# Where the edge counts of a two-layer graph kernel are made: in the second loop, or ahead of it

## The reference, cut to what matters

```python
h = relu(layernorm(x))
Q, K, V = h @ Wq + bq, h @ Wk + bk, h @ Wv + bv          # 8 heads of 16
scores = sum(Q[dst] * K[src], -1) * scale + (edge_attr @ We + be)
p = exp(scores - segment_max(scores, dst)[dst])
x = x + (segment_sum(p * V[src], dst) / segment_sum(p, dst)) @ Wo + bo

h = relu(layernorm(x))
h = logmap0(h) @ W.T + b
deg = count(dst) + count(src);  dinv = deg ** -0.5
out = segment_sum(h[src] * dinv[src] * dinv[dst], dst)
x = x + expmap0(out)
```

## Time and profile before

| what | value |
|---|---|
| median of 3 runs | 884.59 us |
| the profiled execution, its span | 885.71 us, 883.5 us |
| PE, PE weight loads | 778.6 us (88%), 604.3 us (68%) |
| DVE, ACT, POOL | 695.8 us (79%), 529.5 us (60%), 558.7 us (63%) |
| first product of the attention sums, of the counted sums | 81.7 us, 652.5 us |
| mean granted clock of PE | 0.942 of full speed |

### The profile page before, as it was taken

One profiled execution on the slowest core, in us unless ns is written; L12 is line 12 of the kernel. 1 busy time (PEld: TensorE's weight loads), 2 busy tenths in 40 slices (PEclk: granted clock), 3 DMA queues, 4 the chain that ended last, 5 costly groups with the idle time before them and its releaser, 6 DMA issues.

```text
span 883.5 us, 20988 instructions
## 1 busy us (share of the span) xinstructions
PE 778.6 (88%) x5179; PEld 604.3 (68%) x5179; DVE 695.8 (79%) x2576; ACT 529.5 (60%) x1376; POOL 558.7 (63%) x581
## 2 busy tenths in 40 slices
PE   5658978999889999999999999987479999999995
PEld 2336756767667777777777777775358888787875
DVE  8846865878657787877877877776999898999984
ACT  4477745666545776766667667642856556464641
POOL 0077775777756777777777777750067767666762
PEclk9958989999979999999999999996789999999998
DMA  5653464555544445445445445442132222222221
GB/s 173 203 150 100 121 126 108 122 131 124 117 94 110 136 122 139 122 127 138 124 125 139 125 124 140 124 110 77 45 83 64 70 57 68 59 71 55 70 57 49
DMA packets 107213, 94.96 MB, mean 107 GB/s; under 512 B 39836, under 2 KB 91265, under 8 KB 107169
## 3 DMA queue, kind: packets, MB, share of 16 engines
q0 software_dynamic: 25088, 65.05, 27.5%
q1 hardware_dynamic: 82089, 29.51, 13.6%
HBM read 83.35 MB, written 11.15 MB: 107 GB/s over the span
## 4 chain that ended last, share of the span: by engine, by line
PE 35%; DVE 22%; issue 14%; POOL 10%; DMA 8%; SPq 5%; ACT 3%; DVEq 2%; POOLq 1%
POOL kv L816 9%; PE ps_q L1852 7%; PE ps_r L1872 5%; PE ps_s L1829 5%; DVE wv L1501 3%; DMA kv<-kv_tab,idx 3%; DMA qwin<-q_tab 3%; DVE fwd_reset L1500 3%; PE ps_r L2030 3%; PE ps_c L1821 2%; PE ps_f L1907 2%; PE ps_s L1839 2%; DVE ST L1500 1%; SPq L593 1%; ACT ST L1621 1%
## 5 line engine op out<-in xcount | busy, mean ns | idle before, releaser
L816 POOL DMA_INDIRECT kv<-kv_tab,idx x416 | 401.4, 965 | 187.9 <-issue 114.4
L859 POOL DMA_INDIRECT kv<-hs_tab,idx x160 | 156.9, 981 | 122.8 <-DMA hs_tab<-qkv 54.2
L1621 ACT ACTIVATE ST<-ps_s,imj 128x512 f32<-128x512 f32 (+1 forms) x128 | 77.1, 603 | 139.4 <-PE ps_s L1839 139.0
L1852 PE MATMUL ps_q<-qwin,ST 128*128 128x128 f32 x832 | 129.5, 298 | 19.1 <-DMA qwin<-q_tab 15.8
L1852 PEld LDWEIGHTS ps_q<-qwin,ST 128*128 128x128 f32 x832 | 111.9, 202 | 30.3 <-issue 26.1
L1092 DVE TENSOR_TENSOR prod<-kv,ps_q 128x512 f32<-128x512 f32 (+1 forms) x128 | 71.9, 576 | 67.9 <-PE ps_q L1852 43.8
L1604 ACT ACTIVATE S<-iota,nloc 128x128 f32<-128x128 f32 x384 | 121.9, 388 | 0.0
L1872 PE MATMUL ps_r<-wv,S 128*128 128x137 f32 x832 | 114.0, 290 | 0.0
L1872 PEld LDWEIGHTS ps_r<-wv,S 128*128 128x128 f32 x832 | 105.7, 196 | 7.5 <-issue 7.0
L1829 PE MATMUL ps_s<-rep_hi,iota_b 128*128 128x512 bf16 x314 | 98.6, 402 | 0.0
L2030 PE MATMUL ps_r<-qkv,xt 128*128 128x128 f32 x800 | 93.1, 277 | 0.7 <-ACT xt L1747 0.7
(11 more groups left out here) (280 smaller groups left out, 1364.5 us busy)
## 6 DMA issues: line engine op xcount, KB each, us to landing
kv<-kv_tab,idx POOLq DMA_INDIRECT x416, 2.8
attr_s<-in_attr SPq DMA_DIRECT2D x32, 192.0 KB
kv_tab<-qkv SPq DMA_DIRECT2D x4, 640.0 KB, 3.4
kv<-hs_tab,idx POOLq DMA_INDIRECT x160
x_tab<-x SPq DMA_DIRECT2D x32, 64.5 KB, 2.3
qwin<-q_tab SPq DMA_DIRECT2D x32, 64.0 KB
xwin<-in_x SPq DMA_DIRECT2D x32, 64.0 KB
xwin<-x_tab SPq DMA_DIRECT2D x32, 64.0 KB
```

The lines of the kernel that those rows point to most:

```text
L816: pool.indirect_dma_start(out=kv[:, b, t, :], out_offset=None, in_=kv_tab, in_offset=bass.IndirectOffsetOnAxis(ap=idx[:, b, t:t + 1], axis ...
L859: pool.indirect_dma_start(out=kv[:, j, t, 0:D], out_offset=None, in_=hs_tab, in_offset=bass.IndirectOffsetOnAxis(ap=idx[:, j, t:t + 1], ax ...
L1621: A.activation(ST[:, b, t0:t1, :], row_index(c), ACT.Abs, bias=imj[:, 0:1], scale=-1.0).then_inc(s_sta, 1)
L1852: mm = M.matmul(ps_q[c % 2][:, (t - t0) * D:(t - t0 + 1) * D], ST[:, b, t, :], qwin[:, b, :], start=True, stop=True)
```

## The change

- The counts of pairs 0 to 11 (`EARLY`) are made in attention steps 6 to 29 (`COUNT_FROM`), half a pair to a step; those of pairs 12 to 15 in the first eight pairs of the second loop (`late_job`).
- In a counting step the five places of filler products are empty and `count_bank` makes four banks, one after the other in ps_s[1]: before the window sums, after the first transpose of c1, after that of bx and after query chunk 1. The fillers stay in the other steps, with more of them at the end (`TAIL`).
- A bank is now 16 target rows by 25 blocks (400 columns), with the block innermost; keys are 24 rows wide (600 columns) and also have the block innermost. A pair takes 38 count products of 50 to 400 columns, 9,600 in all. Lane one-hots are made for eight tiles in one operation, with the tile innermost.
- ACT copies each bank to one of two stages (`evict`), SP stores it to `counts_tab` in DRAM (`store_bank`). The second loop loads a whole pair's counts, 128 x 3,200 f32, two pairs ahead into one of three buffers (`load_counts`), and `counted_sums` reads its 25 matrices as `rows[:, :, i]`.
- `hs_t` moves from qkv to xt, and the tables for keys and lanes are made between steps 5 and 6 (`run_tables`); the six one-word loads and the stores that feed them move from turns 3 to 11 to turns 2 to 5.
- Between the loops row statistics are taken earlier, and the inverse roots in two calls. The second loop is written out in place of a loop instruction.

The diff, cut to its core:

```diff
 BUSY = (1, 1, 2, 3, 3)
+TAIL = (8, 6, 6)
-W = 28
+W = 24
...
+EB = 16
+CB = P // EB
+KEYS = NT * W
+BANK = NT * EB
+RING = 8
+MADE = [("n", 0)] + [("k", t) for t in range(0, 6)] + [("n", 1)] + [("k", t) for t in range(6, T1)]
+FIRST_KEYS = [range(0, 6), range(10, 14)]
+NEXT_KEYS = [range(6, 10), range(14, T1)]
+COUNT_FROM = 6
+EARLY = 12
+LATE = GROUPS // 2 - EARLY
+HALFBANKS = CB // 2
...
+        ring = qkv[:].rearrange("p a c d -> p (a c d)").bitcast(BF16)
+        oh_node = hT[:].rearrange("p a d -> p (a d)").bitcast(BF16).rearrange("p (a k t) -> p a k t", a=2, t=RING)
+        stage = xn[:].rearrange("p a d -> p (a d)")[:, 0:2 * BANK].rearrange("p (a w) -> p a w", a=2)
...
+            def store_bank(p, k):
+                wait_apart(sp, s_cntc, CB * p + k + 1, (s_base, 1))
+                sp.dma_start(counts_tab[bass.ds(p * P, P), k * BANK:(k + 1) * BANK], stage[:, k % 2, :]).then_inc(s_cst[k % 2], 16)
+
+            def load_counts(m):
+                for i in range(2):
+                    sp.wait_ge(s_cst[i], 16 * HALFBANKS * (m + 1))
+                sp.dma_start(counts[m % 3], counts_tab[m * P:(m + 1) * P, :]).then_inc(s_cld[m % 3], 16)
...
-                def turn(g, b):
+                def turn(g, b, job=None):
                     load_attr(g, b)
                     load_queries(g, b)
+                    if job:
+                        for k in range(HALFBANKS):
+                            store_bank(job[0], HALFBANKS * job[1] + k)
                     store_nodes(g - 2, b)
                     load_nodes(g, b)
...
                 product(0)
                 for c in range(NCH):
+                    if c == 1 and job:
+                        keys(job[0], FIRST_KEYS[job[1]])
...
+            def keys(p, tiles):
+                past = max(LASTBANK[t + RING] + 1 - CB if t < RING else LASTBANK[t - RING] + 1 for t in tiles)
+                if not (known(p) and CB * p + past <= 0):
+                    dve.wait_ge(s_cnt, CB * p + past)
+                for t in tiles:
+                    V.tensor_scalar(oh_key(t), iota_key[:], run_col(src_key, p, t), None, ALU.is_equal).then_inc(s_ohr, 1)
+
+            def lanes(p, h):
+                if not (known(p) and p == 0):
+                    dve.wait_ge(s_cnt, CB * (p - 1) + 1 + LASTBANK[RING * (h + 1) - 1])
+                V.tensor_tensor(oh_node[:, h], run_col(src_lane, p, RING * h, RING).unsqueeze(1).to_broadcast([P, P, RING]),
+                                rep_lane, ALU.is_equal).then_inc(s_ohr, 1)
...
                 if edges:
                     scan_partitions(g, b, A)
+                if job and job[1] == 0:
+                    lanes(job[0], 1)
                 if nodes:
                     carry(g - 1, 1 - b, B)
...
                     if far:
                         set_idx(g + 2, b, s_idx)
+                    if job:
+                        keys(job[0], NEXT_KEYS[job[1]])
+                        if job[1] == 1 and not (known(job[0]) and job[0] == EARLY - 1):
+                            lanes(job[0] + 1, 0)
                     scan_partitions_back(g, b, A)
...
+            def evict(job, k):
+                p, bank = job[0], HALFBANKS * job[1] + k
+                act.wait_ge(s_cnt, CB * p + bank + 1)
+                if not (known(p) and p == 0 and bank < 2):
+                    act.wait_ge(s_cst[bank % 2], 16 * (HALFBANKS * p + bank // 2))
+                A.copy(stage[:, bank % 2, :], ps_s[1][:, 0:BANK]).then_inc(s_cntc, 1)
...
+            def count_bank(job, i):
+                p, k = job[0], HALFBANKS * job[1] + i
+                pe.wait_ge(s_ohr, NMADE * p + READY[k])
+                if not (known(p) and p == 0 and k == 0):
+                    pe.wait_ge(s_cntc, CB * p + k)
+                for t in TOUCH[k]:
+                    e0, e1 = max(ROW0[t], EB * k), min(ROW0[t] + W, EB * (k + 1))
+                    mm = M.matmul(ps_s[1][:, NT * (e0 - EB * k):NT * (e1 - EB * k)], oh_node[:, t // RING, :, t % RING],
+                                  oh_key(t)[:, NT * (e0 - ROW0[t]):NT * (e1 - ROW0[t])],
+                                  start=t == TOUCH[k][0], stop=t == TOUCH[k][-1])
+                mm.then_inc(s_cnt, 1)
...
-            def counted_sums(n):
-
-                pe.wait_ge(s_cntc, CB * (n + 1))
+            def counted_sums(n, job):
+
+                pe.wait_ge(s_cld[n % 3], 16 * (n // 3 + 1))
+                rows = counts[n % 3].rearrange("p (e h) -> p e h", h=NT)
                 for i in range(NT):
-                    M.matmul(sums[0], counts[:, i, :], hs_t[:, i, :], start=(i == 0), stop=False)
+                    if i == NT // 2 and job:
+                        count_bank(job, 0)
+                    M.matmul(sums[0], rows[:, :, i], hs_t[:, i, :], start=(i == 0), stop=False)
+                if job:
+                    count_bank(job, 1)
                 carried(2 * n, 0)
```

More of the change, by code:

```diff
@@ L473, in build @@
         s_cntc = sem("s_cntc")
+        s_cst = [sem(f"s_cst{i}") for i in range(2)]
+        s_cld = [sem(f"s_cld{i}") for i in range(3)]
+        s_restl = sem("s_restl")
         s_xw1 = [sem(f"s_xw1{i}") for i in range(4)]
@@ L1226, in settle, with step @@
                     add_counts(g - 1)
-            def step(g, b, edges=True, nodes=True, more=True, far=True, old=True):
+            def step(g, b, edges=True, nodes=True, more=True, far=True, old=True, settled=False, job=None):
                 A = Steps(nc, dve, s_dA, NA * g)
@@ L1521, in pair @@
                 st = Steps(nc, dve, s_d1, N1 * n)
+                job = late_job(n)
+                if job:
+                    keys(job[0], FIRST_KEYS[job[1]])
                 window(2 * n, 0, 2 * j, st, more)
+                if job:
+                    if job[1] == 0:
+                        lanes(job[0], 1)
+                    keys(job[0], NEXT_KEYS[job[1]])
+                    if job[1] == 1 and job[0] + 1 < DG:
+                        lanes(job[0] + 1, 0)
                 if far:
-                    for t in range(T1):
-                        run_one_hots(n + 2, t)
                     dve.wait_ge(s_g1[j], 8 * T2 * (n + 2 - j))
@@ L1544, in _ @@
             with dve.If_eq(in_order, 1):
-                for n in range(2):
-                    for t in range(T1):
-                        run_one_hots(n, t)
+                lanes(EARLY, 0)
                 shift1(0, 0)
                 shift1(1, 1)
-                pair(0, 0)
-                pair(1, 1)
-                with dve.Fori(1, DG // 2 - 1) as m:
-                    pair(2 * m, 0)
-                    pair(2 * m + 1, 1)
-                pair(DG - 2, 0, far=False)
-                pair(DG - 1, 1, more=False, far=False)
+                for n in range(DG):
+                    pair(n, n % 2, more=n + 1 < DG, far=n + 2 < DG)
             with dve.Else():
@@ L1739, in one_hots1 @@
                     A.activation(S[:, j, t0:t1, :], S[:, j, t0:t1, :], ACT.Relu, bias=1.0, scale=-1.0).then_inc(s_S1, 1)
-            def count_copies(n, banks):
-                if 0 in banks and not (known(n) and n == 0):
-                    act.wait_ge(s_agg1, 2 * n - 1)
-                for k in banks:
-                    act.wait_ge(s_cnt, CB * n + k + 1)
-                    A.copy(counts[:, :, BANK_ROWS[k][0]:BANK_ROWS[k][1]], bank_rows(k)).then_inc(s_cntc, 1)
             with act.If_eq(in_order, 1):
@@ L1948, in _ @@
                 step(0, 0, nodes=False)
[L1949 to L1952 removed]
+                for g in range(1, COUNT_FROM):
+                    step(g, g % 2)
+                step(6, 0, job=(0, 0))
+                step(7, 1, job=(0, 1))
+                with pe.Fori(4, 14) as n:
+                    step(2 * n, 0, job=(n - 3, 0))
+                    step(2 * n + 1, 1, job=(n - 3, 1))
+                step(28, 0, job=(EARLY - 1, 0))
+                step(29, 1, job=(EARLY - 1, 1))
+                pe.wait_ge(s_cntc, CB * EARLY)
                 step(GROUPS - 2, 0, far=False)
```

369 lines of the change are left out of this document (187 added, 182 removed).

## The result

| | before | after |
|---|---|---|
| median | 885.24 us (4 runs, 882.42 to 886.65) | 958.07 us (4 runs, 953.39 to 968.73) |
| profiled span | 883.5 us | 951.0 us |
| PE, DVE busy | 88%, 79% | 88%, 70% |
| mean granted clock of PE | 0.942 | 0.923 |

The changed kernel is slower: ratio 1.0824, 95% interval 1.0774 to 1.0874. One of its four executions (968.73 us, granted clock 0.906) fell into a slower state of the chip, and ratios leave such executions out. The forecast was 923 us, with 866 to 940 as its range: the direction and the main mechanism were right, the time was 35 us short and outside the range.

The account below looks back on a forecast made before the run. PE was taken to pace attention steps, later POOL's gathers, and PE and DVE the second loop's pairs. Span 883.5 + 16 (attention) + 22.7 (second loop, -3.5 between loops included) = 922.2, +2.2 around it = 924.4, given as 923 us; range 866 to 940.

Parts of the forecast that it names:

- The sum's weights: Second loop: spread f32 weights load at half rate, 303 ns a load, 11.1 us a sum (5.6 to 11.9); chance 0.54.
- spread weights load free: Rival, second loop: spacing costs nothing, POOL's 12.6 us a pair is the pace, 875 us in all; chance 0.34.
- A pair without counting: Second loop, the eight pairs without a late count: 14.7 us each with the 11.1 us sum, over the gathers' 12.6.
- The first eight pairs also carry half a late count, 19 products, +2.4: 17.1: Second loop: late counting adds 2.4 us to 14.7, making 17.1 us a pair.
- so I give it no time: Second loop: SP's 1.6 MB count loads a pair cost nothing, the DMA engines' share being 0.25.
- About even: Attention loop, PE: 10 dropped fillers (2.1 to 2.5 us) against 19 gained count products (2.2 to 2.8 us).
- The counting step: Attention steps 6 to 29: 16.8 us each, 0.5 over the gathers' pace, +12 us in all (0 to +36).
- No row prices three; I take no change: Attention loop: six one-word loads, three in a row on SP's queue, cost 0, between -5 and +10 us.
- The table step: Between attention steps 5 and 6: making the tables on DVE's path once costs +4 us net (+3 to +6).
- the rival of 986 us: Count products' spread lane weights load slowly too, 222 ns a product, +2.0 us in each of 24 steps; chance 0.07.
- Between the loops: Row statistics moved under the last step, one rsqrt chain becoming two: -3.5 us, between -6 and +2.
- the tail: After the last carry of the second loop: its 9.2 us stays unchanged.

Follow-up runs that it names:

- keys_ahead: Changed kernel; in counting pairs DVE makes the next half job's first keys ahead of the norm, and ACT the tanh right after eviction 0: 954.29 us, ratio 1.0672.
- one_product: Changed kernel, each attention-loop bank of counts made with its covering tile's product alone (counts incomplete, only time meant): 1079.39 us.
- one_filled: one_product with two fillers of 512 columns ahead of each bank in the attention loop: 948.92 us.
- laid: Changed kernel, transposed edge numbers as laid-out inputs in four plain loads; flat stores, one-element loads and rest loads gone: 930.95 us, ratio 1.0554.
- before_laid: Kernel before the change, with the transposed edge numbers laid out as inputs: 866.98 us, ratio 0.9806.

## Why the prediction was wrong, point by point

In the spans the forecast was 922.2 us and the measurement 951.0: 28.8 us short, 12.4 of them in the attention loop and 16.1 in the second loop. The other 6 us of the 35 come from the profiled execution being the shortest of its four (953.39 us against the median of 958.07) and from how span and median were put together.

- **The sum's weights: right, and nearly in size.** Forecast 303 ns a load, 222 ns a pass, 11.1 us a sum; measured 335, 241 and 12.06, just above the bound of 11.9. Two rows of other shapes carried this, and the rival "spread weights load free" (0.34) is refuted in both kernels. A pair without counting: 14.7 forecast, 14.58 measured. Its parts were not both right, and it was luck that they cancelled: the sum was 1 us longer and the rest 1 us shorter than allowed for.
- **First failed step: "The first eight pairs also carry half a late count, 19 products, +2.4: 17.1".** Measured 18.5 a pair, 9.9 us over pairs 1 to 7. The work was right: in keys_ahead, at full clock, PE is busy 17.15 us a pair. What the step put at nothing were waits. PE stands still for 7.5 us in these seven pairs, 4.7 for keys that DVE makes behind norm and tanh and 2.8 for evictions, and works 2 us longer at a granted clock of 0.96. With the keys ahead the waits for them fall to 0.7 us and the second loop by 4.4.
- **Second failed step: "so I give it no time", of the counts' loads.** Pair 0 ended 25.0 us after the first gather, 18.7 forecast: 6.3 us. Its last gather is issued at 681.70 and its gathered sum starts at 689.86, 8.2 us later where 2.7 was forecast, beside loads that hold the DMA engines' share at 0.88 (312 GB/s, 670 to 690 us). No run left these loads out, so that they are the cause is argued, not shown. In steady pairs nothing shows.
- **Third failed step: PE's clock has no term in the attention loop.** "About even" weighed the count products against the fillers by their time alone. The trace of the kernel after has three dips in steps 7 to 30 that cost 10 us together, the trace before none from 270 us on. one_product and one_filled show that what PE is given in the fillers' place holds its clock.
- **The counting step: 16.8 forecast; without the dips 16.8 measured** (laid, the 21 steps of 7 to 29 with none), 12 us over the 374.5 that these 23 steps take in before_laid. Right. In the table above the stretch shows only +3.1, because it also lost its transfers.
- **The six one-word loads, "No row prices three; I take no change": wrong in its place, and right in the sum by luck.** The flat stores that came with them were not priced at all. At the start the transfers cost 24 us, far above the bound of +10. But the kernel before paid 21 us for its own, in steps 4 to 11, which the prediction didn't see either, so the net is about +2. The trace before had the price in it: its four steps with such transfers are 20 to 26 us long where the others are 16, 24 us in all.
- **The table step: +4 forecast (3 to 6), +6.7 to +7.3 measured.** DVE's work was 4.7 us, PE's wait 4.1; behind the gap the products ran at the lower clock (0.63 from 180 to 190 us).
- **Lane weights: the rival of 986 us is false.** They are some 50 ns slower each, far from the 222 ns a product of the rival, and mostly hidden: all weight loads together fill 38.62 us of the attention window of 50, PE's products 46.63. The Trainium skill ("TensorE: Matmul & The Clock Gate", Weight-path perf modes) lets 128 non-fp32 weights load fast packed or spread; spread ones took 152 ns here and contiguous ones 97, so not wholly.
- **Between the loops -3.5, measured -2.4; the tail 9.2, measured 8.4.** Right.

## What to carry to other kernels

Float32 weights whose neighbours lie 16 bytes or more apart took 1.6 to 1.9 times as long to load here, 8 bytes apart no longer than adjacent ones (198 ns against 192): choose the innermost index of a stored table by who will read it as weights. When transfers or a block of one engine's work are moved, price them from the steps that hold them now, and add what PE's clock loses behind the gap. Price also what moves away: here the two prices nearly cancelled. Ahead of moving work off a loop, look for the loop's next pace (here 12.3 us of gathers against 13.9 in the mean): that difference is all that can be gained, some 25 us in 16 pairs, and the other loop paid as much.

## What the runs showed of the hardware that was not expected

- Fewer matmuls can make a kernel slower: four fifths of the count products (two thirds of their columns) taken out of the attention loop cost 1079 - 958 = 121 us, at a granted clock of 0.69 in place of 1.00 from 400 to 450 us; 1,024 filler columns a bank, worth nothing to the result, brought it back to 949.
- An ACT copy of 3,200 float32 read 100 bytes apart took 6.17 us, and read in runs of 64 bytes 2.86 us.
- Evicting a PSUM bank of 400 float32 in transposed order (source 100 bytes apart) took 475 ns in the median, and 476 in order: there the spacing cost nothing.
